# Router logits of four tiles kept on four partition ranges and turned back by one full transpose

## The reference

```python
x = x + conv_ref(ln_c(x), ...)              # a gate per image and channel, from mean, max, std and a median
t = to_tokens(x)                            # 2048 x 512
h = ln_t(t)
logits = h @ router_w.T                     # 2048 x 8
top_vals, top_idx = top_k(logits, 1)        # one expert per token
out = sum over e of dense_w[:, e] * glu(h, w1[e], v1[e], w2[e])     # silu(h w1) * (h v1) @ w2
out = out + glu(h, shared_gate.T, shared_up.T, shared_down.T)       # for all tokens
x = from_tokens(t + out)
```

## Time and profile before

| what | value |
|---|---|
| time, median of three executions | 409.06 us (407.67 to 409.27) |
| time of the profiled execution | 408.12 us |
| its span, first to last instruction | 406.4 us |
| TensorE busy | 384.3 us |
| VectorE busy | 255.8 us |
| ScalarE busy | 160.8 us |
| GpSimd busy | 137.3 us |
| mean granted clock of TensorE | 0.982 of full speed |

### The profile page before, as it was taken

How to read it: one execution, slowest core, us unless ns; L and a number is a source line. 1 busy time by engine, 2 the same in 40 slices (tenths; PEclk the granted TensorE clock), 3 DMA queues, 4 the chain that set the end, 5 groups by cost and what they waited for, 6 DMA issues and landing times.

```text
span 406.4 us, 6811 instructions
## 1 busy us (share of the span) xinstructions
PE 384.3 (95%) x1976; PEld 305.4 (75%) x1979; DVE 255.8 (63%) x501; ACT 160.8 (40%) x274; POOL 137.3 (34%) x195
## 2 busy tenths in 40 slices
PE   5864999999999999999999999999999999999994
PEld 2421688887876788888888888888888888888883
DVE  6888776746575676869865557456365654676222
ACT  3876546446511124331115353154264415354110
POOL 7689333300000111106040344426425442545201
PEclk9969799999999999999999999999999999999999
DMA  8900040011110722342340578636646772752300
GB/s 309 413 8 0 26 156 27 26 53 52 53 52 27 284 79 78 99 151 96 123 131 26 185 242 325 233 84 252 220 156 234 290 254 88 267 182 74 93 31 30
DMA packets 14764, 55.96 MB, mean 138 GB/s; under 512 B 2575, under 2 KB 2575, under 8 KB 11280
## 3 DMA queue, kind: packets, MB, share of 16 engines
q1 hardware_dynamic: 9936, 40.93, 28.1%
q0 software_dynamic: 4800, 14.69, 10.1%
HBM read 43.02 MB, written 13.63 MB: 139 GB/s over the span
## 4 chain that ended last, share of the span: by engine, by line
PE 86%; DVE 5%; ACT 4%; POOL 2%; issue 2%; DMA 1%; DVEq 0%; POOLq 0%; ACTq 0%
PE GU L1516 47%; PE yb L1516 23%; PE th L1508 4%; PE tx L1501 4%; PE th L1545 2%; DVE search_junk L903 1%; ACT x_sb L593 1%; DMA x_sb<-x_tok 1%; PE mb L1516 1%; ACT scratch L611 1%; PE mb L1494 1%; ACT scratch L607 1%; PE th L1373 1%; PE yb L1553 0%; ACT w_parts L626 0%
## 5 line engine op out<-in xcount | busy, mean ns | idle before, releaser
L1516 PE MATMUL GU<-w_parts,xT 128*128 (+1 forms) x864 | 214.5, 396 | 0.2 <-DVE xT L1080 0.2
L1516 PEld LDWEIGHTS GU<-w_parts,xT 128*128 128x128 f32 x864 | 158.0, 188 | 31.5 <-DVE xT L1080 0.4
L1516 PE MATMUL yb<-w_parts,hT 128*128 (+1 forms) x420 | 102.8, 393 | 0.0
L1516 PEld LDWEIGHTS yb<-w_parts,hT 128*128 128x128 f32 x420 | 77.8, 188 | 15.6
L660 ACT ACTIVATE hT<-th 128x512 fp32r<-128x512 f32 x36 | 21.5, 597 | 159.5 <-PE th L1508 159.5
L533 POOL DMA_INDIRECT out<-x_sb,scatidx x20 | 37.3, 1866 | 92.7 <-DVE x_sb L1306 83.5
L1071 DVE TENSOR_TENSOR w_parts<-w_raw,w_parts 128x2048 f32 (+1 forms) x24 | 54.9, 2288 | 7.4 <-issue 7.2
L583 ACT ACTIVATE w_parts<-w_raw 128x2048 f32 (+1 forms) x24 | 45.2, 1911 | 4.1 <-issue 4.0
L1055 DVE TENSOR_TENSOR hidden<-hidden,GU 128x512 f32<-128x512 f32 x36 | 24.7, 687 | 34.4 <-PE GU L1516 34.3
L1049 DVE TENSOR_TENSOR hT<-th,hT 128x512 fp32r<-128x512 f32 x36 | 24.8, 689 | 28.0 <-ACT hT L660 27.7
L496 POOL TENSOR_TENSOR x_rstd<-x_mv,eps 128x1 f32<-128x1 f32 x16 | 3.0, 190 | 99.9 <-DVE x_mv L1019 99.9
(11 more groups left out here) (278 smaller groups left out, 349.6 us busy)
## 6 DMA issues: line engine op xcount, KB each, us to landing
w_raw<-weights SPq DMA_DIRECT2D x27, 1024.0 KB, 5.3
x_sb<-x_tok SPq DMA_DIRECT2D x8, 512.0 KB, 7.7
xn_d<-tiles SPq DMA_DIRECT2D x16, 256.0 KB, 2.0
z_d<-x_sb SPq DMA_DIRECT2D x16, 256.0 KB, 2.0
tiles<-xn_d,tokidx POOLq DMA_INDIRECT x20, 4.6
x_sb<-z_d,tokidx POOLq DMA_INDIRECT x20, 5.5
out<-x_sb,scatidx POOLq DMA_INDIRECT x20, 6.8
conv<-conv_par SPq DMA_DIRECT2D x1, 10.0 KB, 6.3
```

Of the source, the lines that this page charges most:

```text
L1516: last = pe.matmul(dst, left[:, lp, kc, :], wset(q, k, wp, kc), start=(i == 0), stop=(i == 3 * KC - 1))
```

## The change

A tile t now writes its 16 rows to partitions 32 x (t mod 4) and up, so that four tiles lie on four ranges of 32 partitions; the buffer changes with every four tiles. The sixteen rows between are whatever the memory held; they end in columns that nobody reads. One transpose of all 128 partitions turns four tiles: in the loop in rounds 2, 6 and 9 (`TURNS`), and one for the last four in the last gate product. VectorE copies four tiles at a time. The wait of TensorE for `logits_used` is kept in those three rounds; a wait for `logits_kept` now stands ahead of the transposes of hidden in every round, counting the tiles routed so far. ScalarE waits for a turn only from tile 8 on, for the turn of the group two before.

```diff
--- before.py
+++ after.py
@@ -36,6 +36,8 @@
 PREPARED = ((), (3,), (4,), (5,), (6,), (7,), (8,), (9, 10), (11, 12), (13, 14), (15,))
 LATE = 6
 SPLIT_AFTER = (8, 9, 10)
+TURNS = {2: 0, 6: 1, 9: 2}
+LAST_TURN = 3
 GATES_IN = {7: 5, 8: 6, 9: 7}
 STORED_GATES = range(1, GROUP)
 
@@ -99,7 +101,7 @@
         powers = sb("powers", [P, 4, B * KC])
         eps = sb("eps", [P, 1])
         steps = sb("steps", [P, SEARCH_STEPS])
-        logits_T = search_junk[0:2 * E, 0:2 * P].rearrange("p (a c) -> p a c", a=2)
+        logits_T = search_junk[:, 0:2 * P].rearrange("p (a c) -> p a c", a=2)
         conv = sb("conv", [P, KC * 5])
         router_w = sb("router_w", [P, KC, E])
         router_parts = sb("router_parts", [P, KC, 2, E], F32R)
@@ -258,13 +260,6 @@
 
             return b + 1 + (b >= GROUP)
 
-        def routed_in(n):
-
-            if n < 0:
-                return (0, 1)
-            held = PREPARED[n - 1][1:] if n else (2,)
-            return held + PREPARED[n][:1]
-
         def tally_second(i):
 
             return mb[:, i:i + 1]
@@ -667,8 +662,11 @@
                 act.activation(gate_rows(b), (th, tx)[b % 2][:, :], ACT.Copy).then_inc(gates_stored, 1)
             def keep_logits(t):
 
+                at = 32 * (t % 4)
+                if t >= 8:
+                    act.wait_ge(logits_turned, t // 4 - 1)
                 act.wait_ge(logits, t + 1)
-                act.activation(logits_T[:, t % 2, :], th[0:2 * E, 0:P], ACT.Copy).then_inc(logits_kept, 1)
+                act.activation(logits_T[at:at + 2 * E, t // 4 % 2, :], th[0:2 * E, 0:P], ACT.Copy).then_inc(logits_kept, 1)
 
             for half in range(2):
                 act.wait_ge(tx_half if half == 0 else tx_done, 1)
@@ -740,7 +738,6 @@
                 if n == 4:
                     scan_second(5)
                 for t in held:
-                    act.wait_ge(logits_turned, t - 1)
                     keep_logits(t)
                 for t in now[1:]:
                     x_hi(t, t % RING)
@@ -1036,13 +1032,11 @@
                 dve.tensor_tensor(xT[:, slot, LO, :, :], tx[:, :].rearrange("p (k t) -> p k t", k=KC),
                                   xT[:, slot, HI, :, :].bitcast(F32), ALU.subtract).then_inc(xlo, 1)
 
-            def take_logits(n, bank):
-
-                tiles_in = routed_in(n - 1)
-                first, many = tiles_in[0], len(tiles_in)
-                dve.wait_ge(logits_turned, tiles_in[-1] + 1)
-                dve.tensor_copy(logit_parts[:, first:first + many, :],
-                                bank[:, 0:many * 2 * E].rearrange("p (t e) -> p t e", t=many)).then_inc(logits_used, 1)
+            def take_logits(g, bank):
+
+                dve.wait_ge(logits_turned, g + 1)
+                dve.tensor_copy(logit_parts[:, 4 * g:4 * g + 4, :],
+                                bank[:, 0:P].rearrange("p (t e) -> p t e", t=4)[:, :, 0:2 * E]).then_inc(logits_used, 1)
 
             def h_lo(n, parity):
                 dve.wait_ge(hhi, n + 1)
@@ -1120,7 +1114,8 @@
                     x_lo(t, t % RING)
                 for t in first if n != LATE else ():
                     norm_tile(t, t % RING)
-                take_logits(n, yb)
+                if n in TURNS:
+                    take_logits(TURNS[n], yb)
                 if n == 4:
                     raise_second(3)
                 h_lo(n, n % 2)
@@ -1188,7 +1183,7 @@
 
             def choose():
 
-                dve.wait_ge(logits_used, len(PREPARED) + 1)
+                dve.wait_ge(logits_used, LAST_TURN + 1)
                 for u in range(RING):
                     dve.wait_ge(xn_out[u], 16 * (NT // RING))
                 own(dve.tensor_tensor(L, logit_parts[:, :, 0:E], logit_parts[:, :, E:2 * E], ALU.add))
@@ -1307,7 +1302,7 @@
                                          op0=ALU.mult, op1=ALU.add).then_inc(y_used, 1)
 
             n = len(PREPARED)
-            take_logits(n, tx)
+            take_logits(LAST_TURN, tx)
             choose()
             h_lo(n, 1)
             lo_of(DOWN, 0)
@@ -1546,11 +1541,10 @@
                                          start=(kc == 0 and lp == HI), stop=(kc == KC - 1 and lp == LO))
                 last.then_inc(logits, 1)
 
-            def turn_logits(n, bank):
-
-                for i, t in enumerate(routed_in(n - 1)):
-                    pe.wait_ge(logits_kept, t + 1)
-                    pe.transpose(bank[:, i * 2 * E:(i + 1) * 2 * E], logits_T[:, t % 2, :], ident[0:2 * E, 0:2 * E]).then_inc(logits_turned, 1)
+            def turn_logits(g, bank):
+
+                pe.wait_ge(logits_kept, 4 * g + 4)
+                pe.transpose(bank[:, 0:P], logits_T[:, g % 2, :], ident[:, :]).then_inc(logits_turned, 1)
 
             def prepare(t):
                 pe.wait_ge(xn_ready, t + 1)
@@ -1622,13 +1616,16 @@
                 if n == LATE:
                     prepare(8)
 
+            routed = 2
             for n, prepared in enumerate(PREPARED):
                 first, second = prepared[:1], prepared[1:]
                 held = PREPARED[n - 1][1:] if n else (2,)
                 gate_product(n + 1, (n + 1) % RING, (n + 1) % 2, 0, 0, lambda: amid_gate(n))
                 if n:
                     pe.wait_ge(y_used, n)
-                turn_logits(n, yb)
+                if n in TURNS:
+                    turn_logits(TURNS[n], yb)
+                pe.wait_ge(logits_kept, routed)
                 transpose_h(n, n % 2)
                 ahead_of_up(n)
                 up_product(n + 1, (n + 1) % RING, (n + 1) % 2, 0, 0, lambda: amid_up(n))
@@ -1638,7 +1635,8 @@
                     pe.wait_ge(hlo, n + 1)
                     route(t, t % RING)
                 ahead_of_down(n)
-                pe.wait_ge(logits_used, n + 1)
+                if n in TURNS:
+                    pe.wait_ge(logits_used, TURNS[n] + 1)
                 down_product(n, n % 2, 0, 0, lambda: amid_down(n))
                 for t in second:
                     prepare(t)
@@ -1647,6 +1645,7 @@
                 for t in first:
                     pe.wait_ge(hlo, n + 1)
                     route(t, t % RING)
+                routed += len(held + first)
 
             def rank():
 
@@ -1670,7 +1669,7 @@
                 last.then_inc(slots_done, 1)
 
             n = len(PREPARED)
-            gate_product(n + 1, 0, 0, 0, 0, lambda: turn_logits(n, tx))
+            gate_product(n + 1, 0, 0, 0, 0, lambda: turn_logits(LAST_TURN, tx))
             transpose_h(n, 1)
             up_product(n + 1, 0, 0, 0, 0)
             rank()
```

## The result

The changed kernel takes **405.52 us** (median of six, 404.48 to 406.35) against 408.65 us of the kernel before beside it (407.61 to 409.27): a ratio of 0.993, interval 0.991 to 0.9949. That is 3.1 us less by the medians, and 0.7% by the ratio; the forecast was 405.2 us, 3.26 us less.

What follows compares the result with a forecast made beforehand. The prediction took TensorE to bound the kernel from about 57 us on; savings place by place summed to 3.26 us, which set against the 408.5 us mean of four executions gave 405.2 us, range 403.8 to 407.4.

Steps and rivals of the forecast that it cites:

- What bounds the kernel: From about 57 us on, a microsecond TensorE no longer spends shortens the span, unless something else is waited for right behind.
- What one small transpose costs: On TensorE, by distances between starts: 0.31 us for a single small transpose, 0.37 us for a pair.
- the rival of the waits: Waits ahead of the small transposes, not the tile, hold the weight load back: gain 1.6 us, 406.9 us; chance 0.20.
- Where it comes from: Weight loads lie bare before and behind the small transpose; all 0.31 us go with the 16-row tile.
- that of the issue alone: Only the small transposes' own matmul time on TensorE goes: gain 0.5 us, 408.0 us, no change; chance 0.06.
- The full transpose: One transpose of 128 rows and columns costs TensorE 0.11 us in the loop, 0.10 in the last gate product.
- n = 1: Round 1, single removed: gain 0.25 us, between 0.17 and 0.31, as VectorE's reduction uses up the slack.
- the signs of being wrong: A load for hidden starting with its matmul, or TensorE newly waiting for a reduction or count at rounds 1, 4, 5.
- n = 3: Round 3, single removed: gains nothing; TensorE waits 0.31 us longer for the count there instead.
- The rest at nothing: Copies of ScalarE and VectorE, moved waits and later stages cost nothing; VectorE could add 1.4 us at most.
- the TensorE sum: Savings on TensorE added place by place over the loop and the last gate product: 3.26 us for the change.
- the third rival: ScalarE's copies to shifted partitions are slow; at 3.1 us each they cost 6.4, ending at 411.6 us; chance 0.04.

Runs made afterwards that it cites:

- e1: The kernel before, its sixteen turns, waits and copies left in place, each turn a full transpose of 128 rows and columns: 407.24 us, ratio 0.9963.
- e3: The kernel before, with the 16-row turns of the loop moved behind the four transposes of hidden: 408.71 us, ratio 0.9997.
- e2: The kernel after, each turn again four 16-row transposes in a row, from four buffers on partitions 0 to 15: 407.72 us, ratio 0.9969.
- e4: The kernel after, with dummy transposes of 16 or 128 rows ahead of those of hidden in rounds 3, 5, 8 and 10: 407.59 us, ratio 0.997.
- e5: The kernel after, first turn in round 3 instead of 2, second behind the transposes of hidden in round 6: 405.38 us, ratio 0.9931.
- e8: The kernel after, one VectorE product of the median search rewritten as comparison and product straight from PSUM: 404.12 us, ratio 0.9908.
- e9: The kernel after with the edits of e5 and e8 together: 403.71 us, ratio 0.9887 to the kernel before.

## Why the prediction was right, point by point

*What bounds the kernel.* Right. The distances on TensorE shrink by 3.21 us, the stage by 3.14, and the routed stage keeps its length. The medians differ by 3.13; that this agrees to 0.01 is luck, since the interval of the ratio allows 2.1 to 3.7 us.

*What one small transpose costs.* Right: 0.31 and 0.37, taken as distances between starts. The matmul's own duration (0.23 us) would have given 16 x 0.23 less 4 x 0.27, 2.6 us, by accident not far off; the 0.17 from its start to the next start would have given 1.6, as in the rival of the waits.

*Where it comes from.* The bare loads belong to the 16-row form (e1), not to the waits (e3), and the price hangs on the number of changes, not of matmuls (e2, e4). The rival of the waits, at 0.20, and that of the issue alone, at 0.06, both fall with e1.

The runs e1, e2 and e4 change the rows and the columns of the small transpose together, and the prediction put the price on the tile as a whole. Two other kinds of matmul in the kernel before tell the two apart. The router's (L1545) have 128 rows, but weights of only 16 columns, tile 128*16:

```profile
90.32 0.84 PE L1516 MATMUL yb<-w_parts,hT 128*128 128x512 f32 x3
...
90.78 0.67 PEld L1545 LDWEIGHTS th<-xT,router_parts 128*16 128x16 f32 x8
91.00 0.63 PE L1545 MATMUL th<-xT,router_parts 128*16 128x128 f32 x8
...
91.47 0.67 PE L1516 MATMUL GU<-w_parts,xT 128*128 128x512 f32 x2
```

The third down matmul starts at 90.78 and the first of the router 0.23 later, a plain step, with its load started at 90.78 under the product; the eight take 0.47 up to the next product, 0.06 each. So this change of tile costs nothing that can be seen. The tally's matmul (L1467) streams a single column, by weights of 128 rows and 128 columns:

```profile
105.35 0.49 PE L1508 MATMUL th<-ident,hidden 128*128 128x128 f32 x3
105.57 0.10 PEld L1467 LDWEIGHTS mb<-counts_bf,same_batch 128*128 128x128 bf16 x1
105.67 0.17 PE L1467 MATMUL mb<-counts_bf,same_batch 128*128 128x1 bf16 x1
...
105.70 0.71 PE L1516 MATMUL GU<-w_parts,xT 128*128 128x512 f32 x2
```

The last transpose of hidden starts at 105.57, the tally's matmul 0.11 later and the product another 0.03 later, 0.14 in all; the small transpose of e3, also behind those of hidden, made 0.37 of the same distance (149.75 to 150.12). So few columns do not bring the price; what is left is the 16 rows. That is read from the trace, and no run changed the rows alone. The late load of L1467 in round 3, which the prediction held in favour of the waits, isn't one of 16 rows and stays unexplained.

The Trainium skill, "TensorEngine Tiling (Array Packing)", section Key Properties, says that a change of tiling mode drains TensorE. The runs agree for the change between 16 and 128 rows, at 0.12 us each; the change to the router's tile shows no such price, and there the measurement decides.

*The full transpose.* Right: 0.11 in rounds 2, 6 and 9 (0.77 against 0.66). In the last gate product the place gave 0.34 where 0.37 was forecast.

*n = 1.* The reduction of VectorE does become the limit. Two lines of the timeline of the kernel after:

```profile
72.61 0.66 DVE L834 TENSOR_REDUCE stats_rows<-mb 128x2 f32<-128x512 f32 x1
...
73.32 0.66 PE L1436 MATMUL mb<-ident,x_sb 128*128 128x128 f32 x4
```

The reduction ends at 73.27 and the transposes into mb follow at 73.32, with a bare load: 0.66 for four, not 0.60. The slack of 0.32 us is used up, 0.09 or so is lost, and 0.21 is left of 0.31; forecast 0.25 between 0.17 and 0.31. TensorE waiting for a reduction at n = 1 also stood among the signs of being wrong, so the prediction counted it twice: as a term of its sum and as a sign against it. It is no more than the term.

*n = 3.* Right: 0.03. Time moved from the transpose into the wait for the count, and e4 and e5 show it from both sides: a small transpose put back costs nothing there, and a full one put there is free.

*The rest at nothing.* Right as far as seen. e1 has all twelve copies of VectorE and all waits of the kernel before, and its stage falls by the TensorE sum alone (1.94 of 2.0). ScalarE's copies to the other partitions take what they took (the kernel after: 250, 266, 268 ns as least, median and most), so the third rival has no ground; a slower copy wasn't tried.

*The number.* 3.26 forecast, 3.14 in the stage, 3.13 between the medians. Working from the mean of the four executions (408.5) and not from the profiled one alone (408.12) was worth 0.4 us, as the profiled execution was one of the shorter ones.

## What to carry to other kernels

Price a small instruction by the distance between the starts of its neighbours, with and without it, not by its duration: on TensorE a matmul of 16 rows among those of 128 cost 0.31 us, a full one of 128 rows and 128 columns 0.11. So fill the partitions, even with rows that nobody reads, and gather small matmuls of one form. Here the unread rows lay in memory that the median search had filled with finite numbers (its comparison results); other contents weren't tried. Then ask of each place whether TensorE waits a little later anyway: one place of twelve gave nothing, and a transpose that is left there is free.

## What the runs showed of the hardware beyond that

The executions of one kernel fall into two clusters: of 35 of the kernel before beside e1 to e4, 16 lie between 407.44 and 408.29 us and 19 between 408.75 and 409.76, none between (of 11 more beside e5, e8 and e9, one does lie between, at 408.38). The instruction that e8 rewrites took 1.05 us in two profiles (before, e5) and 2.27 to 2.29 in five (after, e1 to e4). The two short ones belong to executions among the shorter of their kernels (408.12 and 404.49 us), the five long ones to longer ones. In both lengths it ends just behind a subtraction of GpSimd on the first weights. The kernel before (VectorE ends at 38.90, the next subtraction starts at 38.77):

```profile
37.85 1.05 DVE L932 TENSOR_SCALAR hidden<-hidden 128x128 f32<-128x128 f32 x1
...
38.77 1.27 POOL L489 TENSOR_TENSOR w_parts<-w_raw,w_parts 128x512 fp32r<-128x512 f32 x1
```

The kernel after (VectorE ends at 40.11, the last subtraction at 40.02):

```profile
37.84 2.27 DVE L928 TENSOR_SCALAR hidden<-hidden 128x128 f32<-128x128 f32 x1
38.76 1.26 POOL L484 TENSOR_TENSOR w_parts<-w_raw,w_parts 128x512 fp32r<-128x512 f32 x1
```

The same line runs once more in the search of the later images, where GpSimd has no subtraction beside it. The kernel before:

```profile
118.12 0.23 DVE L932 TENSOR_SCALAR w_raw<-w_raw 128x128 f32<-128x128 f32 x1
```

So VectorE's product, 0.23 us by itself, ended with one subtraction or with two, and the same product read from PSUM took 0.35 us beside the same subtractions. The Trainium skill, "SBUF — State Buffer", section Who interferes with whom, says that a VectorE instruction in a two-port mode, which a `tensor_scalar` can enter, and a GpSimd one contend for a shared pair of ports, which the one that issues first holds for its whole instruction. The ends above agree; the runs show neither the mode nor a port. It isn't the whole of the scatter: two of e8's six executions (405.30 and 405.46) still lie 1.1 us and more above the other four, while e9's five lie within 0.44. TensorE's granted clock ahead of the first gate product differs between executions too (digits 6 and 7 in the third and fifth slice of before, 9 and 8 after); what part that has stays open.
